# Eighteen token tiles in the first expert part instead of twenty, the last four routed three slots sooner from SBUF

## What is computed

```python
x = _layernorm(x + _L0_attn_ref(x, wq, wk, wv, wo))
# the routed part, xt = x as 4096 rows of 512
logits = jnp.clip(xt @ gate_w.T, -50.0, 50.0)          # 8 experts
top_w, top_idx = jax.lax.top_k(logits, 2)
rw = jax.nn.softmax(top_w, axis=-1)
weighted = (jax.nn.softmax(expert_atom_weights) @ atoms) * jax.nn.sigmoid(importance)
rows, cols = mask_idx // H, mask_idx % H               # 4096 entries
vals = jnp.einsum('tk,tks->ts', rw, weighted[top_idx])
contrib = segment_sum((xt[:, cols] * vals).T, rows, num_segments=H)
out = xt @ W.T + contrib.T
x = _layernorm(x + out)
```

## Time and profile before

| | |
|---|---|
| median of three runs | 1840.94 us (1840.28 to 1843.01) |
| the profiled execution | 1839.99 us, span 1838.2 us |
| TensorE busy | 1776.5 us (97% of the span), granted clock 0.989 |
| VectorE, ScalarE, POOL busy | 1236.2, 814.6, 798.7 us |
| from span's start to slot 0 of the expert stage | 1552.64 us |
| last matmul ends | 1805.1 us |

### The profile page before, as it was taken

The page is one execution under the profiler, slowest core; times in us unless marked ns, Lnnn a source line. Parts: engine busy times, 40 slices in busy tenths (PEclk is TensorE's granted clock), DMA queues, the critical chain, the costliest instruction groups (busy, mean ns, idle before and its releaser), DMA issues.

```text
span 1838.2 us, 33411 instructions
## 1 busy us (share of the span) xinstructions
PE 1776.5 (97%) x9290; PEld 1502.2 (82%) x9290; DVE 1236.2 (67%) x3881; ACT 814.6 (44%) x2059; POOL 798.7 (43%) x1092
## 2 busy tenths in 40 slices
PE   8999999999999999999999999999999999999992
PEld 7888888888888888888888888888888887777771
DVE  5566467766777577757775777577766776763256
ACT  4444344434444345534453444444544443333344
POOL 6775445534454333333332333233322334676563
PEclk9999999999999999999999999999999999999996
DMA  9655443335333455454545454544445338545688
GB/s 328 232 216 195 164 141 122 120 99 167 115 116 110 161 160 158 146 174 142 158 147 168 132 159 154 176 146 150 149 143 208 115 126 322 189 167 167 239 312 324
DMA packets 157391, 317.93 MB, mean 173 GB/s; under 512 B 23088, under 2 KB 66256, under 8 KB 146704
## 3 DMA queue, kind: packets, MB, share of 16 engines
q1 hardware_dynamic: 138912, 275.83, 44.6%
q0 software_dynamic: 18288, 39.80, 7.1%
HBM read 227.30 MB, written 88.28 MB: 172 GB/s over the span
## 4 chain that ended last, share of the span: by engine, by line
PE 84%; DVE 4%; issue 4%; DMA 3%; POOL 2%; ACT 2%; DVEq 0%; ACTq 0%; POOLq 0%; SPq 0%
PE psum L1547 23%; PE psum L1549 22%; PE psum L1548 22%; PE psum L1574 7%; PE psum L2309 2%; DMA token_rows<-x,ids_now 2%; PE psum L2311 2%; PE psum L2310 2%; PE psum L372 1%; ACT probs L1824 1%; PE psum L794 1%; DVE pT_lo L1948 1%; POOL expert_weights L1443 1%; POOL probs L1423 0%; POOL expert_slots L649 0%
## 5 line engine op out<-in xcount | busy, mean ns | idle before, releaser
L1423 POOL TENSOR_SCALAR probs<-probs,row_inv 128x128 f32<-128x128 f32 (+3 forms) x512 | 307.9, 625 | 433.0 <-DVE row_inv L1945 431.1
L1824 ACT ACTIVATE probs<-probs,neg_max 128x512 f32<-128x512 f32 (+3 forms) x512 | 282.5, 554 | 360.6 <-DVE neg_max L1937 358.5
L1547 PE MATMUL psum<-xT_hi,w_hi 128*128 128x512 f32 x640 | 252.4, 394 | 0.7 <-DVE qT_lo L1962 0.7
L1937 DVE CUSTOM_DVE_ANT_0 probs<-psum,causal 128x512 f32<-128x512 f32 (+3 forms) x512 | 223.2, 486 | 42.1 <-issue 20.3
L1549 PE MATMUL psum<-xT_hi,w_lo 128*128 128x512 f32 x640 | 250.1, 391 | 0.0
L1548 PE MATMUL psum<-xT_lo,w_hi 128*128 128x512 f32 x640 | 249.7, 390 | 0.0
L1948 DVE TENSOR_TENSOR pT_lo<-psum,pT_hi 128x512 fp32r<-128x512 f32 (+1 forms) x384 | 206.2, 592 | 20.1 <-ACT pT_hi L1834 20.0
L1834 ACT CAST pT_hi<-psum 128x512 fp32r<-128x512 f32 (+1 forms) x384 | 172.3, 526 | 64.9 <-PE psum L1574 64.9
L1547 PE MATMUL psum<-wo_hi,oT_hi 128*128 128x512 f32 x496 | 196.7, 396 | 0.0
L1549 PE MATMUL psum<-wo_hi,oT_lo 128*128 128x512 f32 x496 | 194.1, 391 | 0.0
L1548 PE MATMUL psum<-wo_lo,oT_hi 128*128 128x512 f32 x496 | 193.5, 390 | 0.0
(11 more groups left out here) (251 smaller groups left out, 3866.4 us busy)
## 6 DMA issues: line engine op xcount, KB each, us to landing
w_hi<-split_qk_weights SPq DMA_DIRECT2D x140, 256.0 KB, 2.7
w_lo<-split_qk_weights SPq DMA_DIRECT2D x140, 256.0 KB, 3.0
wo_hi<-split_out_weights SPq DMA_DIRECT2D x27, 1024.0 KB, 5.4
wo_lo<-split_out_weights SPq DMA_DIRECT2D x27, 1024.0 KB, 7.6
expert_weights_hi_lo<-split_expert_weights SPq DMA_DIRECT2D x8, 2048.0 KB, 9.6
x_in<-in_L_attn_x_dram SPq DMA_DIRECT2D x8, 1024.0 KB, 7.5
expert_weights<-fill SPq DMA_DIRECT2D x16, 512.0 KB, 4.3
attn_residual<-y_acc SPq DMA_DIRECT2D x8, 1024.0 KB, 4.7
```

Of the source, the lines that this page charges most:

```text
L1423: last = pool.tensor_scalar(p, p, row_inv[:, buf, i:i + 1], 1.0, ALU.mult, ALU.mult)
L1547: pe.matmul(dst, hi_s, hi_m, start=start, stop=False)
L1824: last = act.activation(probs[:, buf, a:a + w], probs[:, buf, a:a + w], ACT.Exp, bias=neg_max[:, buf, i:i + 1], scale=-1.0, accum_out=row_ ...
L1937: last = dve.tensor_tensor_reduce(probs[:, buf, a:a + w], psum[:, BANK_S + bank, col:col + w], causal[:, T - w:T], -1.0, -MASKED, ALU.add, ...
```

## The change

FIRST_T is 18. All that hangs on it moves: FULL_TILES 33 to 29, FIRST_DONE 47 to 43, COUNTED 26 to 23. The four last token tiles are routed from slots 0, 5, 10 and 15, straight from `y_acc` in SBUF; their rows are no longer stored and loaded again. The steps of the second part's table are spread over slots 1, 6, 11 and 16. The fifth tile (tile 4) is gathered in attention's last iteration, and POOL then gathers five tiles ahead; ScalarE copies ids one tile further ahead, but those of tiles 29, 30 and 31 together in slot 25. Pairs 0 to 8 begin at slots 46 + 2u; pairs 9, 10 and 11 at 66, 68 and 70. SP waits for the rows of 63 tiles before it loads pair 9. The core of the diff:

```diff
-FIRST_T = 20
+FIRST_T = 18
...
-PAIRS = FIRST_T // 2 + 2
+PAIRS = FIRST_T // 2 + 3
...
@@ def fetch
+    if j <= GROUP:
+        number = pool.value_load(E.tile_number_i[0:1, j:j + 1], min_val=0, max_val=FIRST_COLS - 1)
+        pool.tensor_copy(E.ids_now[:, k:k + 1], E.first_ids[:, bass.ds(number, 1)]).then_inc(E.s_first_ids_now, 1)
+    if j <= GROUP:
+        pool.wait_ge(E.s_first_ids_now, j + 1)
     else:
-        number = pool.value_load(E.tile_number_i[0:1, j:j + 1], min_val=0, max_val=FIRST_COLS - 1)
-        pool.tensor_copy(E.ids_now[:, k:k + 1], E.first_ids[:, bass.ds(number, 1)]).then_inc(E.s_ids_now, 1)
-    pool.wait_ge(E.s_ids_now, j + 1)
+        pool.wait_ge(E.s_ids_now, j - GROUP)
...
 def rows_now(R, tt):
-    return R.row_bufs[own(tt)]
+    if isinstance(tt, int) and tt >= LAST:
+        return R.y_acc[:, tt - LAST]
+    return R.row_bufs[0][:]
...
@@ attention, sync
-        sp.wait_ge(s_y_acc, TT + NIT * TT)
-        sp.dma_start(r_store[NB - 1], y_acc[:]).then_inc(s_r_out, 16)
         ready(range(1, NE))
-        sp.wait_ge(s_r_out, 16 * NB)
+        sp.wait_ge(s_r_out, 16 * (NB - 1))
@@ attention, gpsimd
+            if kind == "end":
+                fetch(pool, R, E, GROUP)
             if route:
                 route_place(pool, R, it - TT)
@@ attention, vector
-                if job == "split" and g == 0:
+                if job == "split" and g == 2:
+                    dve.tensor_copy(R.counts[2][:], R.counts[1][:]).then_inc(s_counts_kept, 1)
+                    wait_apart(dve, s_counts_kept, b - SPLIT_BATCHES[0] + 1, s_passed)
                     dve.tensor_copy(R.counts[1][:], R.counts[0][:])
@@ experts
-    FIRST_ROUTED, ROUTE_STEPS, FIRST_PAIR, PAIR_STEPS, PAIR_END, STORED_LATE, GATED = 3, 5, FIRST_DONE + 5, 2, 6, 4, 3 * GROUP
+    FIRST_ROUTED, ROUTE_STEPS, FIRST_PAIR, PAIR_STEPS, PAIR_END, STORED_LATE, GATED = 0, 5, FIRST_DONE + 3, 2, 6, 4, 3 * GROUP
+    def slot_of(u):
+        if u < FIRST_T // 2:
+            return FIRST_PAIR + PAIR_STEPS * u
+        return SECOND_DONE + 3 + PAIR_STEPS * (u - FIRST_T // 2)
+    def ids_of(j):
+        k = j + GROUP + 2
+        if FULL_TILES <= k and j < COUNTED + 2:
+            return ()
+        return tuple(range(FULL_TILES, k + 1)) if j == COUNTED + 2 else (k,) if k < JT else ()
@@ experts, sync
-        ask_rows(LAST)
-        ask_rows(LAST + 1)
         for tt in range(LAST, NT):
             route_store(sp, R, tt, R.x1_dram[tt * P:(tt + 1) * P, :])
-            if tt + 2 < NT:
-                ask_rows(tt + 2)
@@ experts, gpsimd
-            if j + GROUP == FULL_TILES:
+            asked = j + GROUP + 1
+            if asked == FULL_TILES:

                 pool.wait_ge(R.s_x1_out, 16 * (NT + 1))
-            if j + GROUP < JT:
-                fetch(pool, R, E, j + GROUP)
+            if asked < JT:
+                fetch(pool, R, E, asked)
@@ experts, vector
-            if j == 0:
+            if j == 1:
+                read_second(dve, E, table, psum, BANK_RANK)
                 bins_first(dve, R, E, table)
-            if j == 1:
-                bins_second(dve, R, E, table, psum, BANK_RANK)
-            if j == 2:
+            if j == ROUTE_STEPS + 1:
+                bins_second(dve, R, E, table)
+            if j == 2 * ROUTE_STEPS + 1:
                 bin_ends(dve, E, table, range(2 * NE, EARLY_BINS))
                 rest_early(dve, E, table)
-            if j == 3:
+            if j == 3 * ROUTE_STEPS + 1:
                 rest_early_sums(dve, E, table)
```

66 lines of the change are left out of this document (28 added, 38 removed).

## The result

The changed kernel takes 1858.3 us (median of 4 runs, 1856.14 to 1861.53), the kernel before 1841.97 us (median of 4, 1840.28 to 1843.19): 0.9% slower, ratio 1.0089 (95% interval 1.0075 to 1.0102). The sign and the range of the prediction held; its centre, 1848.5, lies 10 us too low. The profiled execution took 1858.56 us and its span 1856.8 us, 18.6 more than the span before.

What follows compares the result with a forecast made beforehand. TensorE's own timeline was taken as the bound; -6.6 + 8.5 + 5.5 - 1.7 + 10.0 - 7.6 = +8.1 us on 1839.99 gave 1848.1, forecast as 1848.5 us. Range 1837 to 1860.

Steps and rivals of the forecast that it cites:

- First term: Slots 0 to 2: asking tile 4's rows in attention removes TensorE's wait and half clock, 6.6 us less.
- Second and third term: Routing three slots sooner delays TensorE up to slot 27, +8.5 us; hand-over to the second part idles it, +5.5.
- Fourth term: Pair stage, gathering five ahead: saves 7.7 us, waits for expert-row stores cost 6; net -1.7, bounds costing 0 to 17.
- Rival (3): Worse: the two-slot store-to-gather cycle holds from slot 46 to 62, costing 16 instead of 6: 1858 us; chance 0.13.
- Fifth term: Behind slot 63: pair 8's sum waits for store 4 behind pair 9's loads; TensorE idles 8.1 us, net +10.0.
- Sixth term: Tail after the last matmul: left pairs wait only for their own loads, 25.5 us instead of 33.1, so -7.6.
- Rival (1): Faster: an unbroken DMA string from the first pair load sets the end, 1835.6 us as a median; chance 0.15.
- Rival (2): No change: no fourth-term cost (-7.7 for -1.7), the blocked sum costs 8 for 10: 1841 us; chance 0.20.
- Rival (4): Early fifth-tile rows help nothing, the sixth's being 3 us late with half clock: 1853 us; 0.52 shared with the forecast.

Runs made afterwards that it cites:

- the fourth run: The kernel before with only tile 4's rows asked in attention, ahead of the two placings (two small-input semaphores merged): 1837.47 us, against 1841.46.
- The seventh run: The change, still eighteen tiles, with all early table steps put back in slots 0 to 3: 1858.16 us.
- the fifth: The change with FIRST_T put back to twenty token tiles and no added wait for the counts, the rest as changed: 1843.66 us.
- the third run: The change with rows asked four tiles ahead instead of five, tile 4 still asked in attention: 1853.43 us.
- the second run: The change without the register-valued wait it adds to VectorE's loop over batches 3 to 6: 1854.70 us.
- the first run: The change with the output store of pair 4 moved ahead of pair 9's blocked loads on the SP queue: 1851.45 us.
- The mended run: The change with store 4 ahead of the blocked loads, no added wait in VectorE's loop, and rows asked four ahead: 1841.67 us.

## Why the prediction was right, and where it was not

**First term (-6.6): right.** Slots 0 to 2 take 9.82 us; the fourth run shows it alone (10.0 us).

**Second and third term (+8.5, +5.5): right.** Slot 22 begins 86.75 us behind slot 0, forecast 86.1. TensorE idles 3.98 us before slot 27, forecast 4.2, and slot 27 is 2.3 us too long (granted clock 0.56 from 1663.1 to 1668.5), where I took 3.2 for the half clock. Slot 34 is 7.3 us behind, forecast 7.4. That tenth is luck: slot 22 comes 0.7 us late and slots 22 to 26 take 0.3 more, and the wait and the half clock give 1.1 back. The seventh run excludes that it is the place of the table steps, the fifth that it is anything but eighteen tiles that opens the hand-over's wait.

**Fourth term (-1.7): within its bounds, its two halves not seen on TensorE.** The gathers' waits for stores are there (up to 3.63 us), but neither the 7.7 us that asking sooner was to save nor the 6 that the waits were to cost shows: TensorE's waits for token rows in these slots are 2.6 us after and 3.1 before, and the third run, four ahead, takes 101.1 us for the change's 100.6. That the row reads -0.2 is within what two executions of one program differ by. Rival (3), that this cycle holds and costs 16, is half right: the sends do fall 4 to 8 us behind from tile 45 on, but over slots 34 to 62 TensorE loses 7.4 us, not 16. What the cycle did cost lies elsewhere, in the next term.

**Fifth term (+10.0): the mechanism right, a size off (+11.6).** The step that failed is "send 62 is issued at +0.95": it was issued at +4.35, since POOL had fallen behind under the fourth term's own gathers. That put 2.9 us on the wait (10.99 for 8.1), and the third run, with four ahead, takes just this away (8.07). Half clock then cost 2.5 us (granted clock 0.54 from 1806.1 to 1811.7), not 3.2.

**Sixth term (-7.6): the step that failed.** I took the time from the first left pair's sum to the last normalization over from before (13.6 us) and let it start at the first load's landing. It was 19.4 us. Before, that stretch was VectorE's own work, not the loads': the first left pair's sum came without a wait, and from the sum of pair 10 to the last left pair's sum VectorE paused once, for 0.67 us. Its two rows with a wait, before:

```profile
1811.14 1.29 DVE L2386 TENSOR_TENSOR c_z<-c_y,c_y 128x512 f32<-128x512 f32 x2 [3.14 <-DMA out_dram<-c_z]
...
1818.22 1.28 DVE L2411 SCALAR_TENSOR_TENSOR c_shift<-c_mean_var,c_rstd 128x1 f32<-128x1 f32 x2 [0.67 <-POOL c_rstd L2260]
```

With pairs 9 to 11 out of the way the loads set the pace: all four left sums wait for their rows. The chain of waits of the kernel after:

```profile
1828.08 7.34 DMA chosen_rows<-y_rows,slot_now
1835.54 0.32 SPq L2210
...
1836.86 7.89 DMA f_y<-chosen_rows
1844.76 0.69 DVE f_y L2387
...
1850.74 0.70 ACT f_y L2348
```

The first load lands in 5 us, but the last four cannot be asked before tile 70's rows are stored, and that store, issued amid the first four loads, took 7.34 us to land; the last load took 7.89 more. The Trainium skill's fit, cited in the fourth term ("DMA: Bandwidth & Descriptors", section "Anatomy of one DMA — SWDGE (gpsimd) path"), gives 2.6 us for such a store: the 2.82 us of tile 62's send in the quiet queue agree, the 7.34 us do not. Before, the same wait for tile 70 stood in SP's queue and cost nothing, since its rows were sent at 1806.10 and the fifth load was issued at 1812.17. From the first load's issue to the end are 29.7 us after and 29.2 before (1809.04 to 1838.2). Only the 4 us between the last matmul and that issue, in which SP had other stores to send, went away: -3.4.

**Attention (0): an unpriced term, +3.3.** I had called the count copies two instructions of 0.2 us a batch. The wait that comes with them costs 1.1 to 1.2 us at each of three returns of the loop, and the second run takes it away. This and the sixth term are most of the 10 us. The range held, but it reached to 1860 for rival (3), whose 1858 the result matches by chance: its 16 us are not there.

**The rivals.** Rival (1) needed an unbroken string of transfers; its share fell to 0.58 because seven pairs' loads, not six, stand behind tile 62, and from the first pair load (1720.72) to the end are 136.1 us, not 115.1. An earlier TensorE does lengthen the tail in the fourth run, where 4.4 of its 6.7 us reached the end; in the first run all 9.2 did. Rival (2) would need nothing of the fourth term's cost and 8 in the fifth; the slots show -0.2 and +11.6. Rival (4), that the fifth tile's rows help nothing, falls with slot 3 at 1565.75. The mended run, 0.1% above the kernel before, shows that eighteen tiles need not cost what they did.

## What to carry to other kernels

Where one engine's total work bounds a stage, moving a step inside it moves the wait and saves nothing; ask first for the step's place outside the stage, and price what is late next on the queues it passes (a store behind loads that wait for a later event stopped three engines here). A load or store order by hand is right for one distance only: the mend that gave 5 to 7 us at eighteen tiles broke the string of transfers at twenty. And for a tail ask first which engine its old length belongs to: the 13.6 us taken over here were VectorE's work, and once that was gone the last of a row of loads, and what must have landed before it is asked, set the end.

## What the runs showed of the hardware that I had not expected

- One more wait with a register's value in VectorE's loop lengthened each return of the loop from 2.5 to 2.8 us to 3.6 to 4.0 us, in twelve of twelve returns, whether by the wait or by the longer code stays open.
- An indirect store of 256 KB, which lands after 2.8 us in a quiet queue (1792.83), took 7.34 us when it was issued (1828.08) amid four loads of 512 KB (from 1827.11).
- Holding 2 MB of stores back behind eight loads of 512 KB let the last of them land 15.2 us behind the first one's issue instead of 15.7, and did not change the time (1839.91 and 1839.73 us).
